# Gated cross-attention with a quantised FFN on one core: queries projected for two batch rows at once, and two PSUM copies moved from ScalarE to VectorE in every second row

## The chip, the cores and the metric

The kernel runs on one core of one Trainium2 chip, in one launch. The metric is device microseconds of one execution. Before the change three runs gave 798.23, 792.31 and 797.61 us, median 797.61 us. Engines are named as in the profile: PE is TensorE's matmul, PEld its weight load, DVE is VectorE, ACT is ScalarE, POOL is GpSimd, SP is SyncE, which here issues DMAs.

## What is computed

The input is `x` of 32 batch rows, each 112 x 256, and a context of 375 x 256 for each. "Row" below always means one of these 32 batch rows.

```
q, k, v = linear(layernorm(x)), linear(ctx), linear(ctx)      # 16 heads of 16
scores  = q k^T ;  probs = softmax(scores / 4)
feats   = mean of scores, mean over queries of max, variance of probs     # one triple per row and head
t       = exp(clip(mlp(feats)))                                # 64 wide, two exact GELUs
out     = softmax(q k^T / (2 t)) v
x       = x + tanh(g_xattn) * (out Wo + bo)
x       = x + tanh(g_ffn) * ffn(layernorm(x))                  # ternary weights, 8-bit activations, SiLU gate
```

So every score matrix passes through two softmaxes: the first gives the features that set a temperature for each row and head, and the second uses it.

## The kernel before

Five instruction streams are written out by hand, one for each engine. `timeline` (L386) calls each engine's own `slot(t)` with t from -16 on; `n, p = divmod(t, 8)`, so row n has eight slots p0 to p7 and each slot takes two of the 16 heads. An engine does its share of a slot in the order in which its `slot` function lists it, and semaphores alone tie the engines together. After the rows comes the FFN (`tile`).

What every slot holds:

- PE: two score products of 375 columns (L1328) into `p_s`, six transposed score products (L1369) for a row that is 26 slots older into `p_t`, in every second slot 24 products with the values (L1348) into `p_o`, and in most slots one piece that goes through the one PSUM tile `p_m`.
- DVE: the statistics of the first softmax of the slot before the last (two BATCH_NORM_STATS2, L907) and the row maxima of this slot (L926). Small copies stand between them.
- ACT: two second exponentials (`pt`, L1187) and two first exponentials (`ex`, L1197) of the slot before.

The pieces that share `p_m` are ordered by the list `ORDER` (L307): third value piece V2, queries Q, first key piece K0, output projection OP, second key piece K1, the back transposes OB, then V0 and V1. `take` lets PE begin a piece only when the piece before it has been copied out of `p_m`.

Rows alternate. In even rows from 2 on (`pair_of`, L345) the MLP for two rows runs: DVE takes a reciprocal (`fa`, L901), PE multiplies with `w1`, and at p6 and p7 ACT runs two GELUs (L1223, L1144) with a table load ahead of the first and another ahead of the next exponential. "Rows with GELUs" are these even rows; the others are odd. While ACT is at the GELUs, PE fills slot p7 of an even row with two value products: V1 of this row and V2 of the next (`roomy_row`, L350; L1458).

The parts that the change touches:

- Queries of row n + 2 are projected in every row n (L1392 to L1400): at p1 in an even row, at p0 in an odd one (`queries_at`, L354). It takes four f32 products of 112 columns from `xnt`, the normalised row after a PE transpose (L1323) and a DVE copy (L923). DVE adds the bias into `qf` (L875) and sums over the queries into `sumq` (L878); POOL splits `qf` into three bf16 parts (L580 to L594); SP sends these to DRAM and back, spread over `qst` (L445, L497).
- Keys of row n + 2 in two pieces, PE at p2 and p4 (L1419). ACT copies each out of `p_m` with the bias and an accumulated sum (`copy_k`, L1122) at p3 and p5; POOL splits them (L563).
- The weighted sums of row n - 4 (`o_acc` in `p_o`) are copied by ACT to `oa` at p4 (L1169), so that PE can transpose them back at p5 (L1428) and DVE can divide by the sums (L891, L895).

## Time and profile before

| | |
|---|---|
| runs before | 798.23, 792.31, 797.61 us, median 797.61 us |
| the profiled execution | 792.8 us |
| its span, first to last instruction | 791.0 us |
| granted TensorE clock over the span | 0.962 |
| first scores to last scores (L926) | 26.3 to 636.1 us |
| an even row, a row with GELUs (408.81 to 429.33) | 20.52 us |
| the odd row behind it (429.33 to 446.84) | 17.51 us |

A row is taken from the start of its first L926 on DVE to the start of the next row's. From row 9 to row 28 the two lengths repeat within 0.02 us. The profiled execution is 1.8 us longer than its span, and lies 4.8 us below the median of the runs.

### The profile page before, as it was taken

To read this page: it belongs to the slowest core of one execution; us is meant where nothing else is said; L and a number is where in the kernel's file an instruction comes from. 1 tells how busy PE (TensorE), PEld (TensorE's weight loads), DVE (VectorE), ACT (ScalarE), POOL (GpSimd) and SP (SyncE) were. 2 spreads that over 40 slices of the span, in tenths; PEclk is the share of its full clock that TensorE was granted. 3 is DMA by queue.
4 is the path that set the end of the run, shared out by engine and by line. 5 is a ranking of instruction groups with operands and counts; after the bars stand their busy time and mean duration, and the time that the engine had idled before them with its cause. 6 is when DMAs were issued, how large, how long until landed. Compare 5 with 4: busy or idle time off the path is not lost.

```text
span 791.0 us, 20866 instructions
## 1 busy us (share of the span) xinstructions
PE 702.7 (89%) x7118; PEld 474.6 (60%) x7127; DVE 708.0 (90%) x1452; ACT 683.9 (86%) x1454; POOL 487.9 (62%) x956
## 2 busy tenths in 40 slices
PE   6567899999999999999999999999999888877896
PEld 4334566666666666667676766676765555533453
DVE  5779899989899999999999999899999776798995
ACT  1578899898999999999999999999999888768883
POOL 4747657667777667676766666767664043245663
PEclk9666899999999999999999999999999899999998
DMA  9997747464668575767455666656664122246688
GB/s 206 204 261 166 197 127 149 109 126 128 154 120 149 124 144 124 145 122 158 123 138 134 134 137 133 128 136 130 124 118 85 39 68 86 71 103 164 160 179 181
DMA packets 148887, 108.50 MB, mean 137 GB/s; under 512 B 56991, under 2 KB 145183, under 8 KB 148767
## 3 DMA queue, kind: packets, MB, share of 16 engines
...
q14 instruction: 48, 0.39, 0.2%
...
## 4 chain that ended last, share of the span: by engine, by line
PE 36%; ACT 35%; DVE 16%; issue 9%; DMA 2%; ACTq 1%; POOL 1%; SPq 0%; DVEq 0%; POOLq 0%
ACT ex L1197 13%; ACT pt L1187 12%; PE p_o L1348 7%; PE p_m L1426 6%; PE p_s L1328 5%; PE p_m L1407 5%; PE p_t L1369 4%; DVE kst L1032 3%; DVE hmax L1035 3%; PE p_m L1415 3%; ACT L1223 3%; ACT L1187 2%; DVE stats L907 2%; PE p_m L1399 2%; DVE nm L926 2%
## 5 line engine op out<-in xcount | busy, mean ns | idle before, releaser
L1197 ACT ACTIVATE ex<-p_s,nm 112x375 f32<-112x375 f32 x512 | 275.8, 618 | 12.3 <-DVE nm L926 11.0
L1187 ACT ACTIVATE pt<-p_t,ct 128x336 f32<-128x336 f32 x488 | 245.8, 577 | 26.7 <-PE p_t L1369 24.5
L907 DVE BATCH_NORM_STATS2 stats<-ex 112x6 f32<-112x375 f32 x512 | 252.5, 535 | 1.4 <-ACT ex L1197 1.3
L926 DVE TENSOR_REDUCE nm<-p_s 112x2 f32<-112x750 f32 x256 | 236.0, 922 | 1.2 <-PE p_s L1328 1.0
L1328 PE MATMUL p_s<-kst,qst 96*112 96x375 bf16 x512 | 154.8, 348 | 13.5 <-ACT ex L1197 7.3
L1369 PE MATMUL p_t<-qst,kst 99*128 99x112 bf16 x1464 | 115.1, 213 | 4.9 <-ACT pt L1187 4.0
L1369 PEld LDWEIGHTS p_t<-qst,kst 99*128 99x128 bf16 x1464 | 91.1, 98 | 44.0 <-issue 19.7
L1407 PE MATMUL p_m<-wv_sb,ctxt 128*128 128x256 f32 (+1 forms) x384 | 106.7, 401 | 4.7 <-DVE va L859 2.9
L1348 PE MATMUL p_o<-pt,va 128*32 128x112 f32 (+1 forms) x3072 | 101.7, 265 | 1.4 <-ACT pt L1187 0.8
L1426 PE MATMUL p_m<-ctxt,wk_sb 128*128 128x375 f32 x240 | 94.6, 518 | 1.7 <-DVE qf L875 1.1
L1328 PEld LDWEIGHTS p_s<-kst,qst 96*112 96x112 bf16 x512 | 67.0, 139 | 45.7 <-ACT ex L1197 34.6
L1348 PEld LDWEIGHTS p_o<-pt,va 128*32 128x32 f32 (+1 forms) x3072 | 70.4, 110 | 29.3 <-issue 27.0
L1407 PEld LDWEIGHTS p_m<-wv_sb,ctxt 128*128 128x128 f32 (+1 forms) x384 | 66.7, 190 | 20.4 <-DVE va L859 10.3
L859 DVE TENSOR_TENSOR va<-p_m,bv_sb 128x256 f32<-128x256 f32 (+1 forms) x96 | 40.0, 417 | 27.4 <-PE p_m L1407 26.6
L1426 PEld LDWEIGHTS p_m<-ctxt,wk_sb 128*128 128x128 f32 x240 | 44.3, 199 | 28.2 <-DVE x L885 7.5
L572 POOL TENSOR_SCALAR kp<-kf 128x375 bf16<-128x375 f32 x63 | 32.8, 521 | 43.9 <-ACT kf L1130 43.9
L578 POOL TENSOR_TENSOR kp<-kf,kp 128x375 bf16<-128x375 f32 x63 | 55.3, 878 | 5.2
L574 POOL TENSOR_TENSOR kf<-kf,kp 128x375 f32<-128x375 f32 x63 | 55.1, 875 | 5.3
L1492 PE MATMUL p_s<-wq,kp 128*128 128x512 bf16 x161 | 41.1, 380 | 12.6 <-DVE kst L1032 10.0
L744 POOL TENSOR_SCALAR kst<-kst 128x1024 bf16<-128x1024 f32 (+1 forms) x28 | 28.9, 1032 | 28.4 <-ACT kst L1257 28.3
L1257 ACT ACTIVATE kst<-kst,hinv 128x1024 f32<-128x1024 f32 (+1 forms) x29 | 32.1, 1115 | 9.0 <-DVE hinv L1042 9.0
L1032 DVE SCALAR_TENSOR_TENSOR kst<-p_s,usc,kst 128x1024 f32<-128x1024 f32 x28 | 35.9, 1282 | 3.6 <-ACT kst L1250 3.3
...
## 6 DMA issues: line engine op xcount, KB each, us to landing
...
```

Source lines behind the costliest of these rows:

```text
L574: nc.gpsimd.tensor_tensor(kf[:, c], kf[:, c], hi, ALU.subtract).then_inc(s_kx, 1)
L578: nc.gpsimd.tensor_tensor(lo, kf[:, c], mid, ALU.subtract).then_inc(s_kp2, 1)
L907: last = nc.vector.bn_stats(stats[:, nb % RING, 2 * pb + i], ex[0:SQ, 2 * (t % 2) + i, :])
L926: nc.vector.tensor_reduce(nm[:, n % RING, 2 * p:2 * p + 2], p_s[t % 2][0:SQ, :, 0:SK], axis=AX.X, op=ALU.max, negate=True).then_inc(s_max, 1)
L1032: nc.vector.scalar_tensor_tensor(out=hh[n % HHRING].rearrange("p (b k) -> p b k", b=2), in0=p_u[:, :, :], scalar=usc[:, n:n + 1], in1=sg[n ...
L1187: nc.scalar.activation(pt[:, (2 * r + i) % 8], st_home(r, i)[:, 0:KC * SQ].rearrange("k (c q) -> k c q", c=KC), ACT.Exp, scale=ct[:, nr % ...
L1197: nc.scalar.activation(ex[0:SQ, 2 * ((t - 1) % 2) + i, :], p_s[(t - 1) % 2][0:SQ, i, 0:SK], ACT.Exp, bias=nm[:, ne % RING, h:h + 1]).then_ ...
L1328: scores = mm(p_s[t % 2][0:SQ, i, 0:SK], qst[n % KRING][0:STACK, h, :], kst[n % KRING][0:STACK, h, 0:SK], start=True, stop=True)
L1348: last = mm(o_acc[VW * i:VW * (i + 1), grp, :], va[ng % VRING][0:KEYS[c], c, 4 * grp + i, :], pt[0:KEYS[c], (2 * (g - 1) + i) % 8, c, :], ...
L1369: last = mm(st_home(r, i)[:, c * SQ:(c + 1) * SQ], kst[nr % KRING][:, h, c * KR:(c + 1) * KR], qst[nr % KRING][:, h, :], start=True, stop= ...
L1407: last = mm(p_m[0:KEYS[ch], 0:D], ctxt[:, v % CRING, k, ch * KR:ch * KR + KEYS[ch]], wv[:, k, :], start=(k == 0), stop=(k == C - 1))
L1426: last = mm(p_m[:, 0:SK], wk[:, k, c * P:(c + 1) * P], ctxt[:, f % CRING, k, :], start=(k == 0), stop=(k == C - 1))
```

## The change

Three things are done.

1. Queries are projected once for two rows, in odd rows from 1 on, at p1: rows n + 2 and n + 3 together, four products of 224 columns. Rows 0 to 2, 9, 10 and 31 are projected alone. The DVE copy for two rows is at p2, the sum over queries apart from it at p3. `xnt`, `qf` get room for two rows. POOL normalises two rows in an even row (p5 and p7) and none in an odd one, and splits two rows' queries at once. The copy of `xnt` that stood at p0 of even rows stands at p0 of odd rows.
2. In even rows from 6 to 30 (`with_gelu`) DVE copies the second key piece, with its bias and sum, at p5.
3. In the same rows DVE copies the weighted sums at p4. In all other rows ACT goes on doing both.

To make room in SBUF, `st2` shares the tile of `st1`, `lt` is clipped in place and one temporary of the guard is dropped; the loads of `xa` and the stores of `qp` stand a slot or more elsewhere in SP's stream.

```diff
+        def projected(n):
+            first = n + Q_AHEAD
+            pair = n > 0 and first + 1 < B and LN_REST not in (first, first + 1)
+            return range(first, first + (2 if pair else 1)) if active("Q", n) else range(0)
...
+        def with_gelu(n):
+            return pair_of(n) and 2 * BACK // SLOTS <= n < B
...
             n, p = divmod(t, SLOTS)
-            x = n + 1 + Q_AHEAD if p == 7 and pair_of(n) else n + Q_AHEAD if p == 0 and not pair_of(n - 1) else B
+            x = n + Q_AHEAD if p == 0 and (n <= 0 or n + Q_AHEAD == LN_REST) else n + 3 if n >= 0 and p == (7 if n % 2 == 0 else 0) and n + 3 != LN_REST else B
...
-            def split_q(b):
+            def split_q(rows):
...
-                nc.gpsimd.tensor_scalar(hi, qf[:, :, :], 1.0, 0.0, ALU.mult, ALU.add).then_inc(s_qx, 1)
+                nc.gpsimd.tensor_scalar(hi, qf[:, of], 1.0, 0.0, ALU.mult, ALU.add).then_inc(s_qx, 1)
                 pool.wait_ge(s_qx, done + 1)
-                pool.wait_ge(s_qs, count(1, b, 1))
+                pool.wait_ge(s_qs, count(1, e, 1))
...
-                if p == queries_at(n) + 1 and 0 <= n + Q_AHEAD < B:
...
-                    nc.vector.tensor_tensor(qf[:, :, :], p_m[:, 0:C * SQ].rearrange("p (c q) -> p c q", c=C),
-                                            bq[:, :].unsqueeze(2).to_broadcast([P, C, SQ]), ALU.add).then_inc(s_qc, 1)
+                if p == 2 and rows:
...
+                    nc.vector.tensor_tensor(qf[:, of].rearrange("p j c q -> p c j q"),
+                                            p_m[:, 0:C * len(rows) * SQ].rearrange("p (c j q) -> p c j q", c=C, q=SQ),
+                                            bq[:, :].unsqueeze(2).unsqueeze(3).to_broadcast([P, C, len(rows), SQ]), ALU.add).then_inc(s_qc, 1)
+                if p == (3 if n > 0 else 2) and rows:
...
+                        nc.vector.tensor_reduce(sumq[:, first % SRING:first % SRING + 2, :], qf[:, :], axis=AX.X, op=ALU.add).then_inc(s_qs, 1)
...
+                if p == 4 and 0 <= m < B and with_gelu(n):
...
+                    nc.vector.tensor_copy(oa[:, :, :], o_acc).then_inc(s_oc, 1)
+                if p == 5 and 0 <= n + K_AHEAD < B and with_gelu(n):
...
+                    nc.vector.tensor_scalar(kf[:, 1], p_m[:, 0:SK], bk[:, 1:2], 0.0, ALU.add, ALU.add,
+                                            accum_out=sumk[:, f % SRING, 1:2]).then_inc(s_kc, 1)
...
-                copying = p in (3, 5) and 0 <= f < B
+                copying = p in (3, 5) and 0 <= f < B and not (p == 5 and with_gelu(n))
...
-                if p == 4 and 0 <= m < B:
+                if p == 4 and 0 <= m < B and not with_gelu(n):
                     act.wait_ge(s_pv, count(4, m, 4))
...
-                if p == queries_at(n) and active("Q", n):
+                rows = projected(n)
+                if p == 1 and rows:
...
-                            last = mm(p_m[:, c * SQ:(c + 1) * SQ], wq[:, k, c * P:(c + 1) * P], xnt[:, k, :], start=(k == 0), stop=(k == C - 1))
+                            last = mm(p_m[:, c * wide:(c + 1) * wide], wq[:, k, c * P:(c + 1) * P], xnt[:, of, k, :], start=(k == 0), stop=(k == C - 1))
```

The order on the engines changes at these places. First DVE in an odd row, from the last value copy of the even row ahead of it (`va` of 119 partitions) to the maxima of p3. Before:

```order
L859 TENSOR_TENSOR va<-p_m,bv_sb 119x16x16 [waits s_v_projected]
L907 BN_STATS stats<-ex 112x6 [waits s_exp1] x2
L926 TENSOR_REDUCE nm<-p_s 112x2 [waits s_scores]
L875 TENSOR_TENSOR qf<-p_m,bq_sb 128x224 [waits s_q_split,s_q_projected]
L878 TENSOR_REDUCE sumq<-qf 128x2 [waits s_q_copied]
L907 BN_STATS stats<-ex 112x6 [waits s_exp1] x2
L926 TENSOR_REDUCE nm<-p_s 112x2 [waits s_scores]
L907 BN_STATS stats<-ex 112x6 [waits s_exp1] x2
L916 COPY ot<-p_s 128x224 [waits s_o_projected,s_ot,s_scores]
L926 TENSOR_REDUCE nm<-p_s 112x2
L907 BN_STATS stats<-ex 112x6 [waits s_exp1] x2
L926 TENSOR_REDUCE nm<-p_s 112x2 [waits s_scores]
```

The same stretch of DVE after the change:

```order
L881 TENSOR_TENSOR va<-p_m,bv_sb 119x16x16 [waits s_v_projected]
L952 BN_STATS stats<-ex 112x6 [waits s_exp1] x2
L968 COPY xnt<-p_s 128x224 [waits s_q_projected,s_xt,s_scores]
L971 TENSOR_REDUCE nm<-p_s 112x2
L952 BN_STATS stats<-ex 112x6 [waits s_exp1] x2
L971 TENSOR_REDUCE nm<-p_s 112x2 [waits s_scores]
L898 TENSOR_TENSOR qf<-p_m,bq_sb 128x2x2x112 [waits s_q_split,s_q_projected]
L952 BN_STATS stats<-ex 112x6 [waits s_exp1] x2
L961 COPY ot<-p_s 128x224 [waits s_o_projected,s_ot,s_scores]
L971 TENSOR_REDUCE nm<-p_s 112x2
L906 TENSOR_REDUCE sumq<-qf 128x4 [waits s_q_copied]
L952 BN_STATS stats<-ex 112x6 [waits s_exp1] x2
```

The query copy has moved from behind the maxima of p0 to behind those of p1, has twice the columns, and the sum now stands a slot further on; a copy of `xnt` has come in ahead of the maxima of p0.

PE in an odd row, from its scores of p1 to the first key product; before, the queries stood a slot earlier and these rows had none:

```order
L1446 MATMUL p_m<-xnt,wq_sb 128x224 [waits s_xt_copied,s_v_copied]
L1446 MATMUL p_m<-xnt,wq_sb 128x224 x3
L1414 MATMUL p_t<-qst,kst 128x112 [waits s_exp2]
L1414 MATMUL p_t<-qst,kst 128x112 x2
L1414 MATMUL p_t<-qst,kst 128x112 [waits s_exp2]
L1414 MATMUL p_t<-qst,kst 128x112 x2
L1364 MATMUL p_s<-ident_sb,ong 128x112 [waits s_exp1,s_o_guarded]
L1373 MATMUL p_s<-kst,qst 112x375
L1364 MATMUL p_s<-ident_sb,ong 128x112 [waits s_exp1]
L1373 MATMUL p_s<-kst,qst 112x375
L1473 MATMUL p_m<-ctxt,wk_sb 128x375 [waits s_ctx3,s_q_copied]
```

The first key product waits for the query copy (`s_q_copied`), which is now one slot away from it, not two.

DVE in an even row at p4 to p6, before:

```order
L885 SCALAR_TENSOR_TENSOR x<-p_m,tg_sb,xm 112x256 [waits s_x2_in_dram1,s_xb,s_o_projected]
L901 RECIPROCAL fa<-fa 112x32 [waits s_feat_chain]
L907 BN_STATS stats<-ex 112x6 [waits s_exp1] x2
L926 TENSOR_REDUCE nm<-p_s 112x2 [waits s_scores]
L907 BN_STATS stats<-ex 112x6 [waits s_exp1] x2
L926 TENSOR_REDUCE nm<-p_s 112x2 [waits s_scores]
L891 RECIPROCAL rl<-p_m 112x16 [waits s_o_back]
```

And after:

```order
L917 SCALAR_TENSOR_TENSOR x<-p_m,tg_sb,xm 112x256 [waits s_x2_in_dram1,s_xb,s_o_projected]
L924 COPY oa<-p_o 128x448 [waits s_o_back,s_pv]
L946 RECIPROCAL fa<-fa 112x32 [waits s_feat_chain]
L952 BN_STATS stats<-ex 112x6 [waits s_exp1] x2
L971 TENSOR_REDUCE nm<-p_s 112x2 [waits s_scores]
L930 TENSOR_SCALAR kf,sumk<-p_m,bk_sb 128x375 [waits s_k_split,s_k_projected]
L952 BN_STATS stats<-ex 112x6 [waits s_exp1] x2
L971 TENSOR_REDUCE nm<-p_s 112x2 [waits s_scores]
L936 RECIPROCAL rl<-p_m 112x16 [waits s_o_back]
```

Two instructions have come in, one ahead of the statistics of p4 and one ahead of those of p5.

## Rows read from the trace of the kernel before

**Rows 1.** The page, busy time of each engine and its share of the span.
```profile
PE 702.7 (89%) x7118; PEld 474.6 (60%) x7127; DVE 708.0 (90%) x1452; ACT 683.9 (86%) x1454; POOL 487.9 (62%) x956
```
**Rows 2.** The page, the chain that ended last, by engine.
```profile
PE 36%; ACT 35%; DVE 16%; issue 9%; DMA 2%; ACTq 1%; POOL 1%; SPq 0%; DVEq 0%; POOLq 0%
```
**Rows 3.** Stretches: us, busy time of each engine, clock; an even row, an odd row, ten pairs.
```profile
408.81:429.33 20.52, 19.40 (x218) 13.81 (x216) 18.84 (x41) 19.23 (x43) 14.23 (x34) 1.00 0.53 126
429.33:446.84 17.51, 17.19 (x199) 12.04 (x198) 17.07 (x34) 16.70 (x42) 12.09 (x23) 1.00 0.63 148
218.64:598.70 380.06, 365.72 (x4120) 258.20 (x4119) 358.19 (x727) 359.18 (x820) 264.05 (x542) 1.00 0.63 133
```
The engines stand in the order PE, PEld, DVE, ACT, POOL; then come the granted clock, the share of the DMA engines and GB/s.

**Rows 4.** DVE's waits in the ten pairs: us in total, times, longest.
```profile
DVE va L859 <- PE p_m L1407: 12.9, 12, 1.3
DVE qf L875 <- PE p_m L1399: 3.1, 10, 0.3
DVE x L885 <- PE p_m L1415: 3.0, 10, 0.3
```
**Rows 5.** Groups by line and shape, whole run: busy us, mean ns, idle before.
```profile
L1173 ACT COPY oa<-p_o 128x448 f32<-128x448 f32 x32 | 18.0, 563 | 1.0 <-PE p_o L1348 1.0
L1130 ACT ACTIVATE kf<-p_m,bk_sb 128x375 f32<-128x375 f32 x60 | 36.6, 611 | 1.8 <-PE p_m L1426 1.2
L1130 ACT ACTIVATION_READ_ACCUMULATOR kf<-p_m,bk_sb 128x1 f32 x60 | 14.3, 238 | 0.0
L875 DVE TENSOR_TENSOR qf<-p_m,bq_sb 128x224 f32<-128x224 f32 x32 | 12.3, 384 | 5.5 <-PE p_m L1399 5.5
L859 DVE TENSOR_TENSOR va<-p_m,bv_sb 128x256 f32<-128x256 f32 x64 | 26.6, 416 | 5.6 <-PE p_m L1407 4.8
```
**Rows 6.** DVE in order of time, even row 20 and odd row 21: start, us.
```profile
412.12 0.39 DVE L875 TENSOR_TENSOR qf<-p_m,bq_sb 128x224 f32<-128x224 f32 x1 [0.31 <-PE p_m L1399]
412.85 0.99 DVE L907 BATCH_NORM_STATS2 stats<-ex 112x6 f32<-112x375 f32 x2
...
426.31 0.43 DVE L859 TENSOR_TENSOR va<-p_m,bv_sb 128x256 f32<-128x256 f32 x1
426.66 0.24 DVE L936 BATCH_NORM_AGGREGATE mv<-st 128x2 f32<-128x6 f32 x2
428.08 0.42 DVE L859 TENSOR_TENSOR va<-p_m,bv_sb 119x256 f32<-119x256 f32 x1 [1.19 <-PE p_m L1407]
...
430.17 0.38 DVE L875 TENSOR_TENSOR qf<-p_m,bq_sb 128x224 f32<-128x224 f32 x1
...
437.21 0.99 DVE L907 BATCH_NORM_STATS2 stats<-ex 112x6 f32<-112x375 f32 x2
438.12 0.92 DVE L926 TENSOR_REDUCE nm<-p_s 112x2 f32<-112x750 f32 x1
438.95 0.99 DVE L907 BATCH_NORM_STATS2 stats<-ex 112x6 f32<-112x375 f32 x2
```
**Rows 7.** PE in order of time, the same rows.
```profile
408.29 1.03 PE L1407 MATMUL p_m<-wv_sb,ctxt 128*119 128x256 f32 x4
409.15 0.46 PE L1369 MATMUL p_t<-qst,kst 99*128 99x112 bf16 x6
...
426.92 1.12 PE L1407 MATMUL p_m<-wv_sb,ctxt 128*119 128x256 f32 x4
...
429.01 1.04 PE L1399 MATMUL p_m<-xnt,wq_sb 128*128 128x112 f32 x8
429.89 0.46 PE L1369 MATMUL p_t<-qst,kst 99*128 99x112 bf16 x6
...
431.07 0.79 PE L1348 MATMUL p_o<-pt,va 128*32 128x112 f32 x24
...
431.95 0.47 PE L1369 MATMUL p_t<-qst,kst 99*128 99x112 bf16 x6
```
**Rows 8.** ACT in order of time, the same rows.
```profile
428.79 1.00 ACT L1187 ACTIVATE pt<-p_t,ct 128x336 f32<-128x336 f32 x2
429.64 1.08 ACT L1197 ACTIVATE ex<-p_s,nm 112x375 f32<-112x375 f32 x2
```

More of the change, by code:

```diff
@@ L323, in emptied @@
             return {
[L324 removed]
+                "Q": (s_qc, count(1, event(b), 1)),
                 "V0": (s_vc, count(3, b, 1)), "V1": (s_vc, count(3, b, 2)), "V2": (s_vc, count(3, b, 3)),
@@ L487, in slot @@
                     sp.dma_start(x2_d[m5], x2[:, m5 % 2, :]).then_inc(s_x2d[m5 % 2], 16)
+                if p == 5 and 0 < f < B and n > 0:
+                    bounce_q(f)
                 if t == FIRST_STACK:
@@ L670, in slot @@
                     nc.gpsimd.tensor_tensor(fd[:, :], fd[:, :], fc[:, :], ALU.mult).then_inc(s_feat, 1)
-                if (p == 5 and n >= 0 or t == X2_AT) and 1 < n + 3 < B:
-                    x = n + 3
+                x = normed(t)
+                if x is not None:
                     pool.wait_ge(s_ln, LN_ALL if x >= LN_REST else 4 * ln_group(x) + 4)
@@ L792, in split_first_q @@
             def split_first_q():
[L794 to L795 removed]
+                lo, mid, hi = (qp[:, 1, i] for i in range(PARTS))
+                chain(nc.vector.tensor_copy(hi, qf[:, 1]), s_qx, 1)
                 dve.wait_ge(s_qs, 1)
[L797 to L799 removed]
+                chain(nc.vector.tensor_tensor(qf[:, 1], qf[:, 1], hi, ALU.subtract), s_qx, 2)
+                chain(nc.vector.tensor_copy(mid, qf[:, 1]), s_qx, 3)
+                nc.vector.tensor_tensor(lo, qf[:, 1], mid, ALU.subtract).then_inc(s_qp2, 1)
             def split_first_k():
@@ L920, in slot @@
                     dve.wait_ge(s_xt, count(1, x, 1))
-                    if x > 0:
-                        dve.wait_ge(s_qmm, count(1, x))
-                    nc.vector.tensor_copy(xnt[:, :, :], ride[t % 2]).then_inc(s_xtc, 1)
+                    if x > 1:
+                        dve.wait_ge(s_qmm, count(1, event(x - 2), 1))
+                    nc.vector.tensor_copy(xnt[:, (x + 1) % 2], ride[t % 2]).then_inc(s_xtc, 1)
                 if 0 <= t < SLOTS * B:
```

97 lines of the change are left out of this document (56 added, 41 removed).

## The prediction

> **What bounds the kernel now.** I read the busy table first. DVE and PE both stand near 90%, ACT at 86% [rows 1], so shares name no bound. The chain that ended last gives 36% to PE, 35% to ACT and 16% to DVE [rows 2]; taken alone, it says that work taken from PE and ACT pays and work given to DVE is cheap. The stretches by row, read next, speak otherwise. From row 9 on the rows repeat in pairs, an even row of 20.52 us and an odd one of 17.51, 38.03 together, all at the full clock (1.00, the 2.4 GHz level). In the odd row DVE is busy for 17.07 of 17.51 us; in the even one all three are close, ACT at 19.23 of 20.52, DVE at 18.84 [rows 3]. Over ten pairs DVE is busy for 358.19 of 380.06 us, so it idles 2.19 us in a pair [rows 3].
>
> Last, DVE in order of time. A slot without a small copy takes it 1.74 us, 437.21 to 438.95: two statistics and one maximum, back to back [rows 6]. Each small copy adds its own length less the some 0.08 us by which the next instruction starts ahead of its end (`va`: 0.43 long, the next 0.35 behind its start). So DVE's time in a pair is a plain sum plus three waits: 1.2 us for the value product V2 at the end of an even row, 0.3 for the queries in an even row, 0.3 for the output projection in an odd one [rows 4, 6]. That is 1.8 of the 2.19; the other 0.4 are gaps of some hundredths, which I leave as they are. DVE is therefore the engine to count on, and a pair after the change is DVE's work plus what is left of its waits.
>
> Here a page bears on the reading. The Trainium skill, "Perfetto Trace Analysis", section "Identifying the Most-Contended Engine", takes the engine of highest occupancy as the one to relieve, but judges TensorE by its weight loads. By that DVE with 90% is the bound and PE with 60% of weight loads is not [rows 1]; rows 6 agree, rows 2 do not. What rows 2 would make of the time is the first rival.
>
> **DVE's work in a pair.** Removed: two query copies with their sums, 412.12 to 412.85, 0.73 each, 1.46 [rows 6]. Added:
> - The query copy for two rows. 224 columns take 384 ns, 256 take 416 [rows 5], so 1.0 ns a column; 448 columns give 0.61, net 0.53.
> - The sum over two rows' queries. No row here prices it alone; copy and sum together took 0.73, so I give it the copy's net 0.53. Bounds: 0.35 and 0.7.
> - The weighted sums, 448 columns, as a plain copy: net 0.53. ACT takes 563 ns for the same [rows 5]; bounds 0.45 and 0.56.
> - The second key piece, 375 columns: 384 + 151 ns, net 0.46. The trace has no DVE instruction that also accumulates; ACT's copy takes 611 ns and a read of the accumulator 238 behind it [rows 5]. Bounds: 0.46 and, if DVE pays ACT's price for the read, 0.70. I take 0.46, from the nearest rows of DVE.
>
> The copies of `xnt` keep their number. The sum is 2.05, so DVE has 0.6 us more work in a pair (0.35 to 1.0 by the bounds).
>
> On the accumulator the Trainium skill has a rule that speaks against the change: "VectorE: DVE Perf Modes", section "Two Vector instructions with no wait between them", says that a Vector instruction with an accumulator output is two instructions. No run here shows it for DVE; with ACT's 238 ns for the second, the sum below would be about 3 us higher.
>
> **DVE's waits in a pair.** The query wait of the even row goes, since that row projects nothing. A new one comes in the odd row, behind the scores of p1, and it is the dearest term. I follow the ring from DVE's V1 copy (426.31) to the query copy. On PE, V2 began at 426.92; through V2, the MLP's last product, ACT's two exponentials (428.79 and 429.64), the scores of p1, the weighted product (431.07) and one transpose it came to 431.95, 5.03 us [rows 7, 8]. There the query pair stands now. Its length: four records of 256 columns took 0.86, 408.29 to 409.15 [rows 7], so eight of 224 take 2 x 0.86 x 224/256 = 1.5. It can't be under the 0.88 of one row's queries (429.01 to 429.89), nor above twice that, 1.76. After the change V2 can begin once V1 is copied, at 426.79, so the queries are done 5.03 + 1.5 later, with 0.05 to hand over, at 433.37: 6.7 us behind 426.66, where V1's copy gave DVE free. ACT has lost two copies in this row and may reach its exponentials sooner; 428.79 stands right behind other ACT work, and I allow up to 0.4. So 6.3 to 6.7 us.
>
> DVE's work in that ring: 426.66 to 430.17 is 3.51 us, less 1.19 idle, 2.32 [rows 6]; one `xnt` copy of net 0.3 and one more slot of 1.74 come in: 4.36. DVE idles for 1.95 to 2.35 there, partly at V2's copy and partly at the query copy. I take 2.0, since ACT's relief is real. The output projection's wait of 0.3 goes: with the sum at p3 DVE comes later to it. Waits: 2.0 in place of 1.8, so 0.2 more.
>
> ACT's 0.56 and 0.85 in an even row [rows 5], and PE's 2 x 0.88 - 1.5 = 0.26, are off that path and count nothing; what hides them is DVE's own sum. If DVE had slack there, they would be the gain of the first rival. POOL splits two rows at once, and its second step waits for the sum at p3; it is busy for 12.09 of an odd row's 17.51 us [rows 3], which covers this. SP issues the same DMAs, some of them a slot later, a row ahead of their use.
>
> **Sum.** +0.6 and +0.2 make +0.8 us in a pair, 38.8 in place of 38.03. Ten such pairs: +8.0. Rows 6 to 8 and 29 to 30 have lone queries or lack a partner: about +1. In two of the even rows DVE has one statistic less at p7, before V1's copy, which now counts: -0.8. In rows 0 to 5 only the queries change; DVE's work falls there and a wait comes, and I take nothing, with 2 us either way. Together +8, so the profiled execution of 792.8 us (span 791.0) would become 800.8. It lies 4.8 us below the median of the three runs; the same +8 on the median of 797.6 gives 805.6, which I forecast. About 1%, 8 us, is what a measurement of this kernel can tell from no change.
>
> **Rivals.**
> *The GELU chain decides.* If the end of an even row hangs on ACT alone, as rows 2 suggest, ACT is rid of about 1.1 us there (0.56 and 0.61 with what they overlap taken off, and part of the read) in 13 rows: -14 us, 783.6. For it: ACT's 19.23 of 20.52 and the wait of 1.2 us at V2, which is PE's lateness behind the GELUs. Against it: V2 waits for V1's copy, and that stands on DVE behind two statistics that start no sooner than the maxima of p7. It holds if the copies at p4 and p5 fall into DVE idle time. Chance 0.18.
> *The late query copy passes on.* The first key product waits for it, ACT's key copy for that product, POOL for the sum; if these lags come round to the next even row, no old wait goes. Then DVE keeps 1.8 less 0.3 and adds 1.0 at the query copy, +0.7, and with 0.6 to 0.8 of work +1.4 a pair, some 12 pairs: +17, 814.6. It decides once DVE's wait at the query copy is over 1 us while the wait at V2 stays at 1.2. For it: POOL's and PE's streams are in order. Against it: a slot behind the queries DVE, not PE, is late. Chance 0.21.
> *Cancelled.* The ring's waits shrink by as much as the work grows, for example because ACT comes to the exponentials 0.8 us sooner: within 4 us of no change, 797.6. Chance 0.22.
> My forecast, +4 to +12, has 0.39.
>
> **Range and chances.** The forecast's own range is 801 to 810. To 787 at the low end it takes in the cancelled case and a part of the first rival; to 817 at the high end most of the second. Faster by over 1% holds the first rival but for its edge, 0.17; slower by over 1% half of the forecast's cases and nearly all of the second, 0.40; the rest, 0.43, within 1%.
>
> **What would show it.** Right: even rows within 0.3 us of 20.5, odd rows at 18.0 to 18.5; DVE waiting some 0.9 us before the query copy in odd rows and 0.9 to 1.2 before V2's copy; no wait left at the output projection; DVE busy for over 36.3 us of each pair; 448-column copies at 0.6 us. Wrong: even rows under 20 us (the GELU chain), DVE waiting less than 0.4 us at the query copy, a query pair under 1.2 us on PE, or a key copy over 0.8 us on DVE.

## The result, and the profile after

Four runs of the changed kernel gave 817.06 to 818.75 us, median 817.91; the kernel before, on the same chip, 797.92 (792.31 to 798.84). The ratio is 1.0266, 95% interval 1.0217 to 1.0315: slower, by 20 us in the medians. The profiled execution took 818.51 us (span 815.5), against 792.8 (791.0) before, so the two traces differ by 24.5 us: before's profiled run was one of its shorter ones.

Page of the kernel after: busy time and share of each engine, and the chain that ended last, the lines that answer to [rows 1, 2].

```profile
PE 711.9 (87%) x7023; PEld 469.9 (58%) x7023; DVE 716.8 (88%) x1466; ACT 678.1 (83%) x1417; POOL 475.5 (58%) x904
PE 35%; DVE 30%; ACT 13%; issue 12%; POOL 5%; DMA 3%; SPq 2%; POOLq 0%; DVEq 0%; ACTq 0%
```

All shares of the span fell; nothing became a saturated engine. In the chain DVE rose from 16 to 30% and ACT fell from 35 to 13%, with PE at 35 (36 before): the end hangs less on ACT and more on DVE.

Stretches of the kernel after, columns as in [rows 3]: even row 22, the odd row 23 behind it, rows 9 to 28.

```profile
467.71:488.67 20.96, 19.04 (x211) 12.74 (x209) 19.46 (x44) 19.24 (x42) 14.21 (x33) 1.00 0.63 152
488.67:507.19 18.52, 17.85 (x195) 12.43 (x196) 17.17 (x34) 16.32 (x39) 11.21 (x19) 1.00 0.49 99
212.53:606.44 393.91, 368.45 (x4037) 251.30 (x4038) 365.17 (x739) 354.96 (x790) 257.17 (x507) 1.00 0.60 130
```

The same twenty rows of the kernel before:

```profile
201.13:581.47 380.34, 366.00 (x4123) 258.48 (x4121) 358.47 (x727) 359.47 (x822) 266.52 (x545) 1.00 0.63 134
```

A pair went from 38.03 [rows 3] to 39.48 us, the even row by 0.44, the odd one by 1.01. Over the twenty rows it is 13.57 us, 1.36 a pair. DVE is busy for 6.70 us more (0.67 a pair) and idle for 28.74 in place of 21.87, 0.69 a pair more. So, counted on DVE, the loss is half work and half waiting. DVE's waits in these rows, after, which answer to [rows 4]:

```profile
DVE qf L898 <- PE p_m L1446: 12.8, 10, 1.3
DVE va L881 <- PE p_m L1454: 10.8, 10, 1.1
DVE x L917 <- PE p_m L1462: 4.0, 10, 0.4
```

Per pair 1.28 for the queries, 1.08 for V2, 0.40 for the output projection: 2.76 in place of 1.90 (the gaps outside these three shrank by 0.17). DVE in order of time, after, even row 22 and odd row 23, as in [rows 6]:

```profile
474.90 0.48 DVE L917 SCALAR_TENSOR_TENSOR x<-p_m,tg_sb,xm 112x256 f32<-112x256 f32 x1 [0.40 <-PE p_m L1462]
475.31 0.61 DVE L924 COPY oa<-p_o 128x448 f32<-128x448 f32 x1
...
477.79 0.60 DVE L930 TENSOR_SCALAR_CACHE_REDUCE kf<-p_m,bk_sb 128x375 f32<-128x375 f32 x1
478.31 0.08 DVE L930 DVE_READ_ACCUMULATOR kf<-p_m,bk_sb 128x1 f32 x1
...
485.46 0.41 DVE L881 TENSOR_TENSOR va<-p_m,bv_sb 128x256 f32<-128x256 f32 x1
485.79 0.24 DVE L981 BATCH_NORM_AGGREGATE mv<-st 128x2 f32<-128x6 f32 x2
487.09 0.42 DVE L881 TENSOR_TENSOR va<-p_m,bv_sb 119x256 f32<-119x256 f32 x1 [1.06 <-PE p_m L1454]
...
490.42 0.92 DVE L971 TENSOR_REDUCE nm<-p_s 112x2 f32<-112x750 f32 x1
492.62 0.62 DVE L898 TENSOR_TENSOR qf<-p_m,bq_sb 128x448 f32<-128x448 f32 x1 [1.28 <-PE p_m L1446]
```

PE over the same stretch, from V2 at the end of the even row to the query pair and what follows it:

```profile
485.93 1.12 PE L1454 MATMUL p_m<-wv_sb,ctxt 128*119 128x256 f32 x4 [0.45 <-DVE va L881]
...
489.17 0.83 PE L1373 MATMUL p_s<-kst,qst 96*112 96x375 bf16 x2
489.93 0.79 PE L1393 MATMUL p_o<-pt,va 128*32 128x112 f32 x24
490.64 0.23 PE L1432 MATMUL p_o<-identb_sb,nmp 112*48 112x112 bf16 x1
490.80 1.78 PE L1446 MATMUL p_m<-xnt,wq_sb 128*128 128x224 f32 x8
492.42 0.46 PE L1414 MATMUL p_t<-qst,kst 99*128 99x112 bf16 x6
```

The pair is projected from 490.80 on, behind the scores and the weighted product of p1; DVE has been free since 491.34 (its maxima of 490.42) and starts at 492.62.

The other part lies ahead of row 9. Row 0, row 7 and rows 0 to 8, after:

```profile
27.53:51.77 24.24, 12.02 (x37) 7.17 (x36) 14.64 (x27) 10.97 (x23) 11.74 (x20) 0.64 1.07 262
169.83:191.31 21.48, 20.75 (x200) 14.76 (x201) 17.68 (x35) 17.20 (x42) 12.59 (x23) 0.84 0.45 96
27.53:212.53 185.00, 153.92 (x1270) 98.97 (x1269) 160.93 (x340) 153.05 (x327) 115.47 (x221) 0.87 0.71 156
```

And before:

```profile
26.32:45.60 19.28, 11.52 (x35) 6.44 (x34) 14.53 (x27) 10.15 (x23) 9.87 (x18) 0.68 1.08 252
163.00:180.60 17.60, 17.28 (x200) 12.13 (x199) 17.23 (x36) 16.80 (x42) 13.01 (x24) 1.00 0.57 126
26.32:201.13 174.81, 150.35 (x1293) 98.98 (x1292) 159.37 (x338) 153.24 (x332) 117.19 (x234) 0.89 0.72 164
```

Rows 0 to 8 lose 10.2 us, 5.0 of it in row 0 and 3.9 in row 7. In row 0 POOL waits for a load, after:

```profile
48.88 1.22 POOL L700 TENSOR_SCALAR xn<-xa,mv,rstd 112x256 f32<-112x256 f32 x1 [7.42 <-DMA xa<-x_dram]
```

It is `x` of row 4, which the change normalises at p7 of row 0; before, that was done at p5 of row 1. The load is issued at 35.97 us and lands 12.7 us later.

### The profile page after: what moved, and what is told of

The parts are those of the page before. It is cut to its first block, busy times and chain, and to the rows that moved or that the text cites. A ratio compares the mean times of both kernels' runs of the same rounds, so it can differ in the third digit from the quotient of the medians.

```text
span 815.5 us, 20539 instructions
## 1 busy us (share of the span) xinstructions
PE 711.9 (87%) x7023; PEld 469.9 (58%) x7023; DVE 716.8 (88%) x1466; ACT 678.1 (83%) x1417; POOL 475.5 (58%) x904
## 4 chain that ended last, share of the span: by engine, by line
PE 35%; DVE 30%; ACT 13%; issue 12%; POOL 5%; DMA 3%; SPq 2%; POOLq 0%; DVEq 0%; ACTq 0%
DVE stats L952 10%; DVE nm L971 8%; PE p_o L1393 7%; PE p_m L1454 5%; ACT ex L1242 5%; PE p_m L1473 5%; PE p_m L1446 4%; ACT pt L1232 4%; PE p_s L1373 4%; PE p_t L1414 3%; PE p_m L1462 2%; POOL kst L773 2%; POOL kst L766 2%; DMA xa<-x_dram 2%; DVE va L881 1%
## 5 line engine op out<-in xcount | busy, mean ns | idle before, releaser
L1242 ACT ACTIVATE ex<-p_s,nm 112x375 f32<-112x375 f32 x512 | 270.0, 595 | 16.6 <-DVE nm L971 16.2
L1232 ACT ACTIVATE pt<-p_t,ct 128x336 f32<-128x336 f32 x488 | 240.0, 553 | 46.3 <-PE p_t L1414 44.6
L1414 PE MATMUL p_t<-qst,kst 99*128 99x112 bf16 x1464 | 117.5, 214 | 5.9 <-ACT pt L1232 3.6
L1373 PEld LDWEIGHTS p_s<-kst,qst 96*112 96x112 bf16 x512 | 62.0, 137 | 47.4 <-ACT ex L1242 41.0
L1539 PE MATMUL p_s<-wq,kp 128*128 128x512 bf16 x168 | 43.1, 387 | 12.1 <-DVE kst L1077 9.9
L609 POOL TENSOR_SCALAR qp<-qf 128x448 bf16<-128x448 f32 (+1 forms) x18 | 9.2, 513 | 63.5 <-DVE qf L898 63.4
```

The lines of the kernel that those rows point to most:

```text
L1232: nc.scalar.activation(pt[:, (2 * r + i) % 8], st_home(r, i)[:, 0:KC * SQ].rearrange("k (c q) -> k c q", c=KC), ACT.Exp, scale=ct[:, nr % ...
L1242: nc.scalar.activation(ex[0:SQ, 2 * ((t - 1) % 2) + i, :], p_s[(t - 1) % 2][0:SQ, i, 0:SK], ACT.Exp, bias=nm[:, ne % RING, h:h + 1]).then_ ...
L1373: scores = mm(p_s[t % 2][0:SQ, i, 0:SK], qst[n % KRING][0:STACK, h, :], kst[n % KRING][0:STACK, h, 0:SK], start=True, stop=True)
L1414: last = mm(st_home(r, i)[:, c * SQ:(c + 1) * SQ], kst[nr % KRING][:, h, c * KR:(c + 1) * KR], qst[nr % KRING][:, h, :], start=True, stop= ...
```

## The experiments

Ratios are to the kernel before, measured beside each run on the same chip; the kernel after has 1.0266. The times of the kernel before spread over more than 1%, so small differences are read from the rows. Row lengths are from each run's profile, rows 22 and 23 (20 and 21 for the kernel before and for even pairs), with one sum over queries in the odd row (the odd rows that need two are 0.06 longer).

| run | ratio, 95% interval | even + odd row, us |
|---|---|---|
| kernel before | 1 | 20.52 + 17.51 = 38.03 |
| kernel after | 1.0266 (1.0217 to 1.0315) | 20.96 + 18.52 = 39.48 |
| pairs only | 1.0208 (1.0152 to 1.0264) | 20.27 + 18.67 = 38.94 |
| copies only | 1.0091 (1.0052 to 1.0130) | 21.26 + 17.39 = 38.65 |
| V1 first | 1.0236 (1.0176 to 1.0295) | 20.45 + 18.67 = 39.12 |
| query copy late | 1.0274 (1.0217 to 1.0330) | 20.97 + 18.33 = 39.30 |
| short sum | 1.0246 (1.0178 to 1.0314) | 20.97 + 18.34 = 39.31 |
| light V0 | 1.0269 (1.0202 to 1.0337) | 20.96 + 18.53 = 39.49 |
| light queries | 1.0167 (1.0101 to 1.0233) | 20.96 + 17.76 = 38.72 |
| load of x early | 1.0245 (1.0170 to 1.0321) | as after |
| early rows mended | 1.0179 (1.0144 to 1.0215) | as after |
| even pairs | 1.0381 (1.0299 to 1.0463) | 21.20 + 17.81 = 39.01, where the clock stayed at 1.00 |
| pairs at p0 | 1.0114 (1.0049 to 1.0179) | 20.11 + 17.70 = 37.81 |
| pairs at p0, key on DVE | 1.0107 (1.0028 to 1.0187) | 20.10 + 17.70 = 37.80 |
| pairs at p0, both on DVE | 1.0159 (1.0096 to 1.0222) | 20.93 + 17.63 = 38.56 |
| pairs at p0, loads ahead | 0.9969 (0.9941 to 0.9997) | 20.11 + 17.70 = 37.81 |
| the same, key on DVE | 0.9978 (0.9946 to 1.0010) | 20.11 + 17.70 = 37.81 |

### The two parts alone

Pairs only:

```diff
         def with_gelu(n):
-            return pair_of(n) and 2 * BACK // SLOTS <= n < B
+            return False
```

> The query part alone: ACT copies the weighted sums and the second key piece again in every row. Theory A (DVE is the bound, and a pair is its work plus its waits): DVE's work in a pair falls by about 0.4 us against before (two lone query copies with sums at 0.73 each go, one copy for two rows at 0.53 and one sum at 0.53 come), the wait at the query copy of 1.28 us stays in the odd row, the even row loses its query copy and wait (about 1.0 us) and ends at 19.5 to 20.0 us, the odd row stays at 18.4 to 18.6; a pair is 38.0 to 38.5, and with the lost time of rows 0 to 8 (10 us) the whole is 805 to 813 us. Theory B (the copies cost DVE nothing, all of the loss is the late query copy that passes on): a pair stays at 39.3 to 39.5, 815 to 819 us. Theory C (ACT's chain of exponentials and GELUs sets the even row): with its two copies back ACT makes the even row as long as before, 20.5, the pair 39.0, 811 to 816 us with DVE waiting for ACT in the even row.

Copies only (in the kernel before, whose queries stay as they were):

```diff
+                if p == 4 and 0 <= m < B and with_gelu(n):
...
+                    nc.vector.tensor_copy(oa[:, :, :], o_acc).then_inc(s_oc, 1)
+                if p == 5 and 0 <= n + K_AHEAD < B and with_gelu(n):
...
+                    nc.vector.tensor_scalar(kf[:, 1], p_m[:, 0:SK], bk[:, 1:2], 0.0, ALU.add, ALU.add,
+                                            accum_out=sumk[:, f % SRING, 1:2]).then_inc(s_kc, 1)
```

> The two copies alone, in the kernel before: queries one row at a time as before, DVE copies the weighted sums and the second key piece in the even rows. Theory A (DVE's sum): 0.53 + 0.53 us more of work in each even row, the output projection's wait of 0.3 us may go, so a pair is 38.7 to 39.1 in place of 38.03 and the whole is 7 to 12 us over before, 805 to 810. Theory C (ACT's chain sets the even row): ACT is rid of 1.1 us there, V1 and the GELUs come sooner, the pair is 37.0 to 38.0, 784 to 798 us. Theory B (the copies cost nothing): 797 to 799. Rows 0 to 5 as before in all of them.

The pair of pairs only is 38.94, +0.91: above theory A's 38.0 to 38.5, just under theory C's 39.0. Copies only is 38.65, +0.62, just under A's 38.7 to 39.1; the even row carries it (21.26 for 20.52). Together they make 1.53; the whole change has 1.45. So the parts add up, and neither hides the other. Even rows, pairs only and copies only:

```profile
462.77:483.04 20.27, 18.96 (x211) 12.84 (x209) 18.50 (x40) 19.70 (x45) 14.09 (x33) 1.00 0.65 155
```

```profile
452.28:473.54 21.26, 19.50 (x218) 13.77 (x217) 19.83 (x44) 18.80 (x40) 14.49 (x34) 1.00 0.51 119
```

With pairs only ACT is busy for 19.70 of 20.27 us, which speaks for theory C in part; that ACT sets the row there is not shown by its share. The copies take DVE from 18.84 [rows 3] to 19.83 us in copies only, and the row grows by three quarters of it.

### Which stretch sets the odd row

Four edits of the kernel after. V1 first:

```diff
+                if p == 7 and roomy_row(n):
+                    copy_v(n - V_LAG, 1)
                 for k in now:
...
                     nc.vector.bn_stats(st2[:, k, :], xt[:, k % 2, :]).then_inc(s_bn2, 1)
-                if p == 7 and roomy_row(n):
-                    copy_v(n - V_LAG, 1)
```

> The kernel after, but at p7 of even rows DVE copies the second value piece V1 ahead of the two statistics for the FFN (0.74 us), not behind them. In the trace of after PE stands idle for 0.45 us (its weight load for 0.69) until this copy before it begins V2, and DVE then waits 1.06 us for V2. Theory A (the waits on the ring V1 copy, V2, query pair are part of the pair's length): V2, the scores of p1 and the query pair come 0.45 to 0.7 us sooner in 11 or 12 pairs, an even row 20.3 to 20.5, the whole 810 to 813 us. Theory D (GELUs and exponentials, not the V1 copy, hold the ring): even row within 0.1 us of 20.95, 817 to 819 us.

The even row fell by 0.51 as theory A said, to 20.45, and DVE's wait for V2 from 1.06 to 0.47, but the odd row behind it grew by 0.15: the wait at the query copy is 1.43 in place of 1.28, so a part is given back there.

Query copy late (`copy_q` is the copy at L898, moved behind the statistics of p2):

```diff
                     last.then_inc(s_bn, 1)
+                if p == 2 and rows and n > 0:
+                    copy_q()
```

> The kernel after, but in rows from 1 on DVE copies the queries behind the two statistics of p2 (0.99 us), not ahead of them. Theory A (DVE is the bound, and its 1.28 us at the query copy are lost): the statistics fill the wait, the wait falls under 0.4 us, an odd row is 17.6 to 18.0 in place of 18.52, and the whole 806 to 811 us. Theory E (the first key product on PE, which waits for this copy, and ACT's key copy and POOL's splits behind it are what makes the odd row long): PE idles 0.7 to 1 us longer ahead of the first key product, the wait comes back at a later slot, and the odd row stays within 0.2 us of 18.5, 816 to 819 us.

A miss for A: the odd row is 18.33, not 17.6 to 18.0, and within E's 0.2 of 18.5. The wait of 1.28 fell to 0.38, and two came in its place, at the copy of `ot` and at the output projection. DVE, odd row 23:

```profile
490.56 0.62 DVE L898 TENSOR_TENSOR qf<-p_m,bq_sb 128x448 f32<-128x448 f32 x1 [0.38 <-PE p_m L1451]
491.39 0.39 DVE L966 COPY ot<-p_s 128x224 f32<-128x224 f32 x1 [0.20 <-PE p_s L1378]
495.19 0.48 DVE L920 SCALAR_TENSOR_TENSOR x<-p_m,tg_sb,xm 112x256 f32<-112x256 f32 x1 [0.29 <-PE p_m L1467]
```

The first key product and the output projection pass through the same tile `p_m` behind this copy, so a later copy makes them late; the wait of 0.29 is at the second of them.

Short sum:

```diff
-                        nc.vector.tensor_reduce(sumq[:, first % SRING:first % SRING + 2, :], qf[:, :], axis=AX.X, op=ALU.add).then_inc(s_qs, 1)
+                        nc.vector.tensor_reduce(sumq[:, first % SRING:first % SRING + 2, :], qf[:, :, :, 0:2], axis=AX.X, op=ALU.add).then_inc(s_qs, 1)
```

> The kernel after, with DVE's sum over queries cut to 2 of the 112 queries where two rows are summed at once (left out: most of that sum, so the first features are not the reference's). It takes about 0.5 us off DVE in an odd row, at p3, behind the query copy, and nothing off PE. Theory A (DVE's work and its waits make the row): odd row 18.0 to 18.1 in place of 18.52, the whole 4 to 6 us under the kernel after. Theory F (PE bounds the odd row: before it was busy 17.2 of 17.51 us there, and the change put 0.65 us more of projection into it, since the even row's lone projection came over): PE is not touched, the odd row stays within 0.15 us of 18.52, the whole within 3 us of the kernel after.

DVE's work in the odd row fell by 0.37 (17.17 to 16.80, less than the 0.5 I had counted) and the row by 0.18: between A and F. Light V0:

```diff
+                    ks = 1 if ch == 0 and row % 2 == 1 and row >= 9 else C
-                    for k in range(C):
+                    for k in range(ks):
```

> The kernel after, with the first value product V0 of the odd rows from 9 on over half of the contraction only (left out: the second of its two products, so the values are not the reference's). It takes about 0.56 us off PE at p6 of an odd row, five slots behind the query pair, where DVE waits for nothing; DVE's work stays. Theory A: odd row within 0.15 us of 18.52, the whole within 3 us of the kernel after. Theory F (PE bounds the odd row): odd row 17.9 to 18.2, the whole 4 to 7 us under the kernel after.

The odd row stayed at 18.53, which speaks against F. PE's busy time fell by only 0.22 (17.85 to 17.63) in place of 0.56, so the test is weaker than planned, but nothing of it reached the row. Light queries, the same cut ahead of the query copy, in the loop around L1446:

```diff
+                        ks = 1 if len(rows) == 2 and n >= 9 else C
-                        for k in range(C):
+                        for k in range(ks):
```

> The kernel after, with the query products for two rows over half of the contraction only, in rows from 9 on (left out: the second of the two products of each half, so the scores are not the reference's). It takes 0.72 us off PE in an odd row ahead of the query copy, where the run with the light V0 took 0.56 off behind it and gained nothing. Theory G (the pieces that pass one after the other through the one PSUM tile p_m, V1 and its copy, V2, the query pair, its copy, the first key piece, the output projection, set the odd row between V1's copy and the output projection's; engines' sums don't): DVE's wait of 1.28 us at the query copy shrinks by 0.6 to 0.7, the odd row is 17.8 to 18.0 in place of 18.52, the whole 5 to 7 us under the kernel after. Rival H (something else holds the odd row at the 18.34 that both the late query copy and the short sum reached, such as ACT's key copy or POOL's splits): odd row at 18.3 or above, at most 3 us gained.

Odd rows of light V0 and of light queries:

```profile
487.88:506.41 18.53, 17.63 (x193) 12.11 (x194) 17.16 (x33) 16.35 (x39) 11.26 (x19) 1.00 0.47 95
```

```profile
481.29:499.05 17.76, 17.08 (x191) 11.67 (x192) 17.16 (x33) 16.35 (x39) 11.25 (x19) 1.00 0.52 104
```

DVE does the same 17.16 us in both. 0.77 us off PE ahead of the query copy takes 0.76 off the row; 0.22 saved behind it, nothing. Theory G holds for what stands ahead of the query copy: the stretch from V1's copy to it, a chain that passes through PE, ACT and DVE, counts in full. Behind it DVE's own work counts too, but only by half (short sum).

### The start

Load of x early:

```diff
+                if t == -9:
+                    load_xa(HOMED)
-                if p == (1 if n % 2 == 0 else 5) and HOMED <= n + 4 < B:
+                if p == (1 if n % 2 == 0 else 5) and HOMED < n + 4 < B:
```

> The kernel after, but SP issues the load of x for row 4 nine slots ahead of the first scores, not at p1 of row 0. In the trace of after POOL waits 7.42 us for this load in row 0 (there it is normalised two rows' worth earlier than in before), PE and DVE behind it, and row 0 takes 24.24 us in place of 19.28. Theory: the load is the whole cause, row 0 is back at 19.0 to 20.5 us and the whole 4 to 5 us under the kernel after (818), 812 to 815. Rival: another transfer or POOL itself is as late (the key stacks and weights that load at the same time), row 0 stays over 22.5 us and the whole within 2 us of the kernel after. The pairs from row 9 on stay at 39.4 to 39.5 us in both.

Row 0 is 18.89 us, so the load was the cause there. The whole is 812.31, but the kernel before stood at 791.54 beside it, and by the ratio little is gained; its interval spans 12 us, so the row is the better witness. Early rows mended has the lone projection of row 9 at p0 as well:

```diff
-                if p == 1 and rows:
+                if p == (0 if n == LN_REST - 3 else 1) and rows:
                     take("Q", n)
```

> The kernel after with two mends outside the pairs: the load of x for row 4 ahead of the first scores, and the lone projection of row 9 at p0 of row 7, as in before. If late load and lone projection are all that rows 0 to 8 lost (10 us in the traces: 185.0 in place of 174.8), row 0 is at 18.8 to 19.5, row 7 at 17.5 to 18.5 in place of 21.48, rows 0 to 8 at 176 to 179 and the whole 808 to 812 us, while pairs stay at 39.47. If row 7 was long because of the granted clock there (0.84) and not because of where the lone projection stands, row 7 stays over 20.

```profile
26.76:46.03 19.27, 11.71 (x37) 6.77 (x36) 14.84 (x27) 9.81 (x23) 10.76 (x18) 0.68 1.09 249
164.73:183.17 18.44, 18.22 (x200) 12.98 (x199) 17.31 (x35) 17.34 (x42) 12.21 (x20) 0.91 0.50 108
26.76:204.39 177.63, 151.97 (x1270) 97.70 (x1269) 160.80 (x339) 152.18 (x327) 114.76 (x219) 0.88 0.73 161
```

Rows 0 to 8 come to 177.6 us; 7.4 of the 10.2 are these two causes; the rest was not followed. Row 7 fell by 3.0, to just within the 17.5 to 18.5 expected, and its granted clock rose from 0.84 to 0.91 (before: 1.00), so place and clock went together here; which of them led is not told apart.

### Where the pair stands

Even pairs put the pair into even rows and leave the odd row none (with the normalising and turning moved to odd rows to match):

```diff
-            return 0 <= n + OF[piece] < B and (piece != "Q" or n <= 0 or n % 2 == 1 or n + Q_AHEAD == LN_REST)
+            return 0 <= n + OF[piece] < B and (piece != "Q" or n <= 1 or n % 2 == 0)
...
-            pair = n > 0 and first + 1 < B and LN_REST not in (first, first + 1)
+            pair = n > 1 and first + 1 < B
```

> Queries of two rows at once as after, but in the even rows (rows 4 and 5 at p1 of row 2, and so on; rows 0 to 3 alone), and ACT makes both copies in every row, as before the change. The odd row then holds no queries at all. Theory F (PE bounds the odd row): odd row 16.6 to 17.0 us, ACT's 16.5 and DVE's 16.4 of work being the next bounds; the even row, with 20.27 in the run of pairs only, gets the pair's 1.4 us on PE and DVE's 1.1 and is 20.7 to 21.3; a pair 37.4 to 38.2, against 38.94 with pairs in odd rows (run pairs only); row 0 and rows 7 and 8 lose nothing, since there x of row 4 is needed no earlier than before and no lone projection stands at rows 9 and 10: the whole 787 to 800 us, as fast as the kernel before or up to 1% faster. Theory A (what counts is DVE's work and waits, wherever the pair stands): the wait of 1.3 us at the query copy comes in the even row instead, a pair 38.7 to 39.2, the whole 800 to 808.

A miss for F. Without any query the odd row is 17.81, longer than before's 17.51, and rows at the full clock make 39.01, in theory A's 38.7 to 39.2. The whole, 823.82, missed both: the granted clock fell in some rows, and rows 9 to 28 take 400.2 us where ten pairs of 39.01 would take 390.1. Two even rows with the same instructions (20 and 22), then a stretch about the start of p7 in the first, and in the second the same stretch and the next one:

```profile
432.71:453.91 21.20, 19.53 (x210) 13.53 (x208) 18.94 (x41) 19.06 (x43) 15.02 (x36) 1.00 0.57 115
471.72:494.49 22.77, 21.10 (x212) 14.47 (x210) 18.94 (x40) 19.38 (x43) 15.22 (x36) 0.93 0.55 116
...
448.50:450.00 1.50, 0.51 (x3) 0.47 (x4) 1.50 (x4) 1.10 (x3) 1.34 (x3) 1.00 0.53 135
487.50:489.00 1.50, 0.49 (x3) 0.45 (x4) 1.50 (x4) 1.10 (x3) 1.34 (x3) 1.00 0.53 136
489.00:490.50 1.50, 1.50 (x7) 0.73 (x7) 0.51 (x2) 1.47 (x3) 1.23 (x4) 0.51 0.76 163
```

PE has as little to do in both rows ahead of the fall (0.51 and 0.49 of 1.50 us), so this alone does not tell why the clock fell in one and not in the other; that stays open.

Pairs at p0 leave the pair in the odd row, but right behind V2, where the lone projection stood before. ACT makes the copies. Both rows of a pair are normalised sooner to match, the sum is at p2, and the load of `x` for row 4 is early as above.

```diff
-            x = n + Q_AHEAD if p == 0 and (n <= 0 or n + Q_AHEAD == LN_REST) else n + 3 if n >= 0 and p == (7 if n % 2 == 0 else 0) and n + 3 != LN_REST else B
+            x = n + Q_AHEAD if p == 0 and (n <= 0 or n + Q_AHEAD == LN_REST) else n + (p + 1) // 2 if n >= 0 and n % 2 == 0 and p in (5, 7) and n + (p + 1) // 2 != LN_REST else B
...
-                if p == 1 and rows:
+                if p == (0 if len(rows) == 2 else 1) and rows:
                     take("Q", n)
...
-                if p == 2 and rows:
+                if p == (1 if len(rows) == 2 else 2) and rows:
```

> Pairs only (ACT makes both copies), but with both rows of a pair normalised and turned a slot or two sooner (p3 and p5, p5 and p7 of the even row), so that PE projects them at p0 of the odd row, right behind V2, and DVE copies at p1 and sums at p2, as in before; the load of x for row 4 is early as in the run on it. Theory G: the query pair no longer stands behind the weighted product and the scores of p1 in the chain, DVE's wait at the copy falls from 1.4 to 0.2 to 0.6 us, and the odd row is 17.4 to 17.9 in place of 18.67; the even row, with one more xnt copy (0.3 us on DVE), 20.3 to 20.6 in place of 20.27; a pair 37.8 to 38.4 and the whole 788 to 800 us, level with before. Rival H (two rows at once cost the odd row 0.65 us of PE wherever they stand, and PE was full there): odd row 18.2 or more, a pair 38.6 or more, the whole 802 or more.

```profile
456.98:477.09 20.11, 18.89 (x210) 13.05 (x209) 18.46 (x41) 19.36 (x44) 13.80 (x32) 1.00 0.57 134
477.09:494.79 17.70, 17.37 (x198) 12.15 (x197) 17.16 (x34) 16.63 (x41) 11.78 (x22) 1.00 0.61 126
```

DVE at V2's copy and at the query copy there:

```profile
475.84 0.42 DVE L883 TENSOR_TENSOR va<-p_m,bv_sb 119x256 f32<-119x256 f32 x1 [1.19 <-PE p_m L1456]
...
478.48 0.62 DVE L900 TENSOR_TENSOR qf<-p_m,bq_sb 128x448 f32<-128x448 f32 x1 [0.47 <-PE p_m L1448]
```

G's numbers came, lower in the even row: 0.47 us of wait in place of 1.4, a pair at 37.81, under the kernel before. DVE's work in the odd row is the same 17.16 as in pairs only, and the row is 0.97 shorter: the place did it. V2's wait stays at 1.19, as before the change. The whole, 803.75, missed G's 788 to 800: rows 0 to 8 took 186.7 us, 11.9 over before, about half of it in row 2 (27.5 us in place of 21.8), in which POOL waited for another load of `x`. The copies on top of it, first with `oa` left to ACT and V1 first, then both by `with_gelu` as in the kernel after:

> As pairs at p0, and in the even rows DVE copies the second key piece (0.53 us net there, 0.85 off ACT), but not the weighted sums, and V1 ahead of the two FFN statistics at p7. In pairs only ACT was busy for 19.70 of an even row's 20.27 us and DVE for 18.50. If ACT's chain to the GELUs holds the even row there, the 0.85 us show in part: even row 19.9 to 20.3, a pair 37.4 to 38.0, the whole 784 to 795. If DVE's 0.53 count in full, as the copies did in the run of copies only (0.61 a pair for both): a pair 38.2 to 38.7, the whole 796 to 804.

> The whole change, both copies on DVE, with the pair at p0 as in the run before, and the early load of x. Against the pairs at p0 with ACT's copies it shows the price of the two copies with the queries' wait out of the way. From the runs so far (copies alone +0.61 a pair, pairs alone +0.91, both +1.44) the two add up almost without touching each other: then it is 0.5 to 0.7 us a pair over the run with ACT's copies, 38.3 to 39.1 a pair, the whole 795 to 807. If the copies cost only because the query pair was late, it is within 0.2 us a pair of that run.

With the key piece alone (and V1 first) the even row is as with ACT's copies, 20.10; with both copies and V1 behind the statistics it is 20.93, the pair +0.75. The even row with the key piece alone:

```profile
457.80:477.90 20.10, 18.85 (x210) 13.06 (x209) 19.05 (x43) 18.90 (x42) 13.76 (x32) 1.00 0.59 134
```

DVE has 0.59 us more work there than with ACT's copies and ACT 0.46 less, and V2's wait is 0.5 in place of 1.2: the key copy fills the time that V1's place gives back, and the row does not move. With both copies PE waits 0.8 us for V1's copy ahead of V2. The key copy without V1 first, and the copy of the weighted sums alone, were not tried. Last, the loads of `x` a row ahead:

```diff
-                if p == (1 if n % 2 == 0 else 5) and HOMED < n + 4 < B:
-                    sp.wait_ge(s_xn, count(1, n + 4 - 2, 1))
-                    load_xa(n + 4)
+                if p == 5 and n % 2 == 1 and n > 0:
+                    for x in (n + 4, n + 5):
+                        if x < B:
+                            sp.wait_ge(s_xn, count(1, x - 2, 1))
+                            load_xa(x)
```

> Pairs at p0 with ACT's copies, mended at its start: the loads of x for rows 5 and on are issued at p5 of the odd row ahead (in the run of pairs at p0, row 2 took 27.5 us, 7.3 of them in which POOL waited for such a load), and the lone projection of row 9 stands at p0 of row 7 as in before. Theory G (where the pair stands in the chain through p_m decides, and what the kernel after lost in rows 0 to 8 is late loads and lone projections): row 2 at 21 to 22.5 us, row 7 at 17.5 to 18.3, pairs at 37.8, the whole 788 to 796 us, 0.3 to 1.3% under before. Rival: rows 0 to 8 stay 8 us or more over the kernel before's 174.8 for another reason (POOL's earlier normalisation delaying its splits, a lower granted clock), and the whole is 798 or more.

> As the run ahead of it, with the second key piece copied by DVE in even rows and V1 ahead of the two FFN statistics at p7. With the late loads that pair of edits left the even row as it was, 20.10 against 20.11: within 3 us of the run ahead of it, pairs at 37.8.

793.49 and 792.39 us with before at 795.78. The first is faster than before by 0.3%, its interval just under 1; the second's takes 1 in. In the first one's trace row 2 is 21.2 us and rows 0 to 8 are 177.7, still 2.9 over before, more than ten pairs save at 0.22 each; why was not followed further. So of the whole change the pairing saves 0.22 us a pair, 2.2 us in ten pairs or 0.3%, if the pair stands where the lone projection stood, and the copies gain nothing here.

## Why the prediction was wrong

805.6 us, 787 to 817, was forecast; 817.9 came. The forecast's own case was +0.8 us a pair; 1.36 came over rows 9 to 28, the price of the rival "the late query copy passes on" (+1.4). Two terms failed: DVE's waits in a pair, and the first rows, put at nothing or little. In the traces rows 9 to 28 cost 13.6 us where 8.0 less 0.8 was forecast, and rows 0 to 8 cost 10.2 where about 1 was, so the first rows hold the larger part of the miss. That the rival's 814.6 lies near the whole is in part luck: it had all of its 17 us in the pairs and nothing in the first rows.

- *DVE's work, +0.6 (0.35 to 1.0): right.* It is +0.67 over rows 9 to 28. The new instructions, kernel after, groups by line and shape:

```profile
L898 DVE TENSOR_TENSOR qf<-p_m,bq_sb 128x448 f32<-128x448 f32 x13 | 8.1, 625 | 14.9 <-PE p_m L1446 14.9
L924 DVE COPY oa<-p_o 128x448 f32<-128x448 f32 x13 | 8.0, 615 | 0.0
L930 DVE TENSOR_SCALAR_CACHE_REDUCE kf<-p_m,bk_sb 128x375 f32<-128x375 f32 x12 | 7.2, 600 | 0.0
L906 DVE TENSOR_REDUCE sumq<-qf 128x4 f32<-128x448 f32 x10 | 6.1, 606 | 0.0
L930 DVE DVE_READ_ACCUMULATOR kf<-p_m,bk_sb 128x1 f32 x12 | 1.0, 82 | 0.0
```

  The 448-column copies were to take 0.61 and take 0.62. The key copy takes 0.60 and an accumulator read of 0.08, 0.52 us net (477.79 to 478.31), within 0.46 to 0.70. The Trainium skill's rule ("VectorE: DVE Perf Modes", section "Two Vector instructions with no wait between them") that an accumulator output makes two instructions holds here: the read is a record of its own, of 82 ns, a third of ACT's 238 [rows 5].
- *The waits, 2.0 in place of 1.8: the step that failed in the pairs.* "I take 2.0, since ACT's relief is real": queries and V2 make 2.36, just above the 2.35 that stood as the upper end. The ring from V1's copy took 6.83 us (485.79 to 492.62) for 6.3 to 6.7. V2 began 0.14 us into it, as forecast; from there to the query pair it took 4.87 in place of 5.03, so ACT's relief brought at most 0.16 of the 0.4 allowed; the pair took 1.62 (490.80 to 492.42) for 1.5 and the step to its copy 0.20 for 0.05, which ate it up. ACT did have time to spare now, but it spent it waiting for PE's last product of the MLP, which stands behind V2, and V2 stands behind V1's copy, for which PE idled 0.45 us:

```profile
487.42 0.29 ACT L1200 ACTIVATE lt<-p_o,b_sb 128x32 f32<-128x32 f32 x1 [0.19 <-PE p_o L1507]
```

  "The output projection's wait of 0.3 goes" failed too: it went from the odd row and came in the even row at 0.40. A likely reason is that DVE, without a query copy there, reaches that copy sooner: in even pairs, whose odd rows have no queries, the wait is 0.7 in the odd row. Idle time is +0.69 a pair, forecast +0.2.
- *The rival's condition came, its route is not shown.* It was to decide once the query wait is over 1 us while V2's stays at 1.2; they are 1.28 and 1.08. But its reason was that the lag comes round to the next even row, and in pairs at p0, where the query wait is 0.47, V2's is 1.19 all the same. V2's wait stays whether the copy is late or not. Its price came because 1.28 us came at the new query copy, and only 0.31 went at the old one and 0.21 at V2.
- *"DVE is the engine to count on": half right.* It gave the work term. But in the odd row 0.37 us less of DVE's work gave 0.18, and 0.77 us less on PE ahead of the query copy gave 0.76. By the Trainium skill ("Perfetto Trace Analysis", section "Identifying the Most-Contended Engine"), which the prediction followed, DVE is the one to relieve; here the chain from copy to copy through one PSUM tile gave more.
- *Rows 0 to 5 at 0, with 2 either way, and 1 for the lone queries: wrong, the other step that failed.* Rows 0 to 5 cost 6.0 us, rows 6 to 8 another 4.2. The sentence at fault is that SP's DMAs stand "a slot later, a row ahead of their use": the load of `x` for row 4 is issued at p1 of row 0 and used at p7, and with it early row 0 is back at 18.89. The lone queries of row 9, a slot later than before, stand in row 7, which lost 3.9.
- *One statistic less, -0.8: right.* The two rows with one statistic, 16 and 24, are 20.63 in place of 20.96, together -0.65. Row 28 is as short, but for another reason: it has both statistics and lacks one copy of `xnt`, since no row is left to normalise. Rows 16 and 28:

```profile
349.54:370.17 20.63, 19.04 (x211) 12.74 (x209) 19.07 (x42) 19.10 (x42) 13.90 (x32) 1.00 0.80 150
585.81:606.44 20.63, 18.62 (x208) 12.40 (x207) 19.13 (x43) 18.91 (x41) 13.13 (x32) 1.00 0.66 144
```
